# Query and key projections of later batches from fp32r parts instead of fp32

## The reference, cut to what matters

```
Q = (query @ Wq.T + bq)          # query = layernorm(x)
K = (key @ Wk.T + bk)            # key = context
scores = einsum('bhqd,bhkd->bhqk', Q, K) / sqrt(16), causal
out = softmax(scores) @ V, then @ Wo.T + bo
x = x + out;   x = x + experts(layernorm(x)) + shared(layernorm(x))
```

## Time and profile before

| | |
|---|---|
| median of three runs | 495.11 us |
| the profiled execution | 494.46 us, its span 492.4 us |
| mean granted TensorE clock | 0.995 of full |
| PE busy, DVE, ACT, POOL | 93%, 63%, 43%, 40% of the span |
| chain that ended last | PE 68%, DVE 15%, ACT 6%, issue 5%, DMA 4% |
| L679, the projections | 64 records; 7% is the largest line of the chain (L628), L679 has 6% |

### The profile page before, as it was taken

How to read it: one execution, slowest core, us unless ns; L and a number is a source line. 1 busy time by engine, 2 the same in 40 slices (tenths; PEclk the granted TensorE clock), 3 DMA queues, 4 the chain that set the end, 5 groups by cost and what they waited for, 6 DMA issues and landing times.

```text
span 492.4 us, 10465 instructions
## 1 busy us (share of the span) xinstructions
PE 457.4 (93%) x3237; PEld 322.0 (65%) x3238; DVE 312.2 (63%) x651; ACT 211.8 (43%) x421; POOL 196.0 (40%) x204
## 2 busy tenths in 40 slices
PE   7979999999999999999978999999999999999992
PEld 6754444654447444564555546699999999999852
DVE  4985757477563856647975895955455555554446
ACT  2255666527572566656764253332332223223210
POOL 4113544214541337302622003036676666665420
PEclk9999999999999999999999999999999999999997
DMA  8593422422124021310398901014444444444389
GB/s 272 101 230 101 126 72 72 140 69 72 63 76 150 32 97 38 115 64 2 98 379 322 327 2 43 0 39 72 76 64 65 74 75 64 65 72 68 36 208 333
DMA packets 45575, 53.86 MB, mean 109 GB/s; under 512 B 7760, under 2 KB 41872, under 8 KB 44912
## 3 DMA queue, kind: packets, MB, share of 16 engines
q1 hardware_dynamic: 34320, 39.77, 25.2%
q0 software_dynamic: 7488, 10.31, 13.3%
q10 hardware_dynamic: 3744, 3.47, 2.7%
HBM read 27.09 MB, written 13.67 MB: 83 GB/s over the span
## 4 chain that ended last, share of the span: by engine, by line
PE 68%; DVE 15%; ACT 6%; issue 5%; DMA 4%; SPq 1%; POOL 0%; DVEq 0%; ACTq 0%; POOLq 0%
PE set_a L628 7%; PE set_b L658 6%; PE set_a L679 6%; PE set_a L934 6%; PE set_a L933 6%; PE set_a L935 6%; PE set_b L648 4%; DVE attention L1317 3%; ACT attention L1084 3%; PE set_b L952 3%; PE set_a L670 3%; PE set_a L842 3%; PE set_b L953 3%; PE set_b L954 3%; PE set_b L943 2%
## 5 line engine op out<-in xcount | busy, mean ns | idle before, releaser
L1317 DVE TENSOR_REDUCE attention<-set_a 128x2 f32<-128x1024 f32 (+2 forms) x96 | 95.9, 1040 | 25.1 <-PE set_a L630 23.0
L1084 ACT ACTIVATE attention<-set_b 128x512 f32<-128x512 f32 (+1 forms) x176 | 87.8, 570 | 50.2 <-PE set_b L648 36.6
L532 POOL TENSOR_SCALAR_AFFINE_SELECT attention<-attention 128x512 f32<-128x512 f32 x64 | 42.6, 679 | 100.5 <-ACT attention L1084 100.5
L592 POOL DMA_INDIRECT sum_rows<-moe,token_of x39 | 61.8, 1585 | 43.9 <-issue 29.8
L648 PE MATMUL set_b<-attention 99*128 99x512 bf16 (+3 forms) x256 | 59.2, 303 | 7.1 <-ACT attention L1084 5.7
L628 PE MATMUL set_a<-attention 96*128 96x512 bf16 (+3 forms) x256 | 60.5, 302 | 4.9 <-DVE attention L1317 4.7
L1184 ACT ACTIVATE moe<-set_a 128x384 f32<-128x384 f32 x39 | 19.1, 490 | 105.2 <-PE set_a L935 95.6
L584 POOL DMA_INDIRECT e_x<-normed_rows,token_of x39 | 39.4, 1011 | 61.3 <-DVE token_of L1516 34.9
L1541 DVE TENSOR_TENSOR moe<-set_a,moe 128x384 f32<-128x384 f32 x39 | 21.7, 557 | 63.0 <-issue 36.3
L628 PEld LDWEIGHTS set_a<-attention 96*128 96x128 bf16 x256 | 24.9, 97 | 44.3 <-DVE attention L1317 17.2
L933 PE MATMUL set_a<-wup_hi,e_xT_hi 128*128 x156 | 53.0, 340 | 0.0
(11 more groups left out here) (169 smaller groups left out, 859.0 us busy)
## 6 DMA issues: line engine op xcount, KB each, us to landing
attention<-attention SPq DMA_DIRECT2D x182, 64.0 KB, 2.6
wup<-in_wupT SPq DMA_DIRECT2D x2, 3072.0 KB, 15.5
sum_rows<-attention SPq DMA_DIRECT2D x2, 2048.0 KB, 13.0
wup<-sum_rows SPq DMA_DIRECT2D x8, 512.0 KB, 7.4
attention<-in_ctxT SPq DMA_DIRECT2D x7, 512.0 KB, 5.6
w_down<-in_wdnT SPq DMA_DIRECT2D x3, 1024.0 KB, 4.9
x_res<-in_x SPq DMA_DIRECT2D x4, 512.0 KB, 6.5
out<-x_res ACTq DMA_DIRECT2D x8, 256.0 KB, 4.0
```

What stands on the lines that cost most here:

```text
L592: g.indirect_dma_start(acc[i], bass.IndirectOffsetOnAxis(token_of[:, t:t + 1], 0), e_y[:, t % 2, :], None, compute_op=ALU.add).then_inc(ad ...
L1084: nc.scalar.activation(pT[k][:, h:h + heads, :], bank(par)[:, 0:heads * (S - k * P)], ACT.Exp).then_inc(b_free, 1)
L1317: v.tensor_reduce(dst, src, AX.X, ALU.max, negate=True).then_inc(a_free, 1)
```

## The change

- Five of the six halves (all but the first, half 0 of batch 0's loop turn) use `project_parts`: for each chunk c, three fp32r products, so 12 matmuls of 128 x 128 by 128 x 512 for queries and keys together, in place of 4 fp32 ones.
- High parts of the rows are made by ACT copies (`rows_high`): batch 1's together with the weights' after the first slot's exponentials, batch 2's ahead of `part1` in slot 3 of batch 0, batch 3's behind slot 0's exponentials. They lie where `w_down_hi` will be, the weights' parts in the last third of `w_down_lo`.
- Low parts are made by POOL subtractions (`rows_low`), written over the fp32 rows: batch 1's behind the masks of slot 1 of batch 0, batch 2's behind those of slot 3, batch 3's behind those of slot 0. The weights' come ahead of all of these.
- PE waits for the low parts (`in_low`) ahead of each such half. The loops of PE, ACT and POOL over batches run from 1 to 2, with batch 0 written out ahead of them.

```diff
+        in_lo = attention_r[:].rearrange("p (a c n) -> p a c n", a=2, c=C)
+        in_hi = wdn_hi[:].rearrange("p b n -> p (b n)")
+        wqk_parts = wdn_lo[:, M - 1, :].rearrange("p (i a c n) -> p i a c n", i=2, a=2, c=C)
...
+            def low_parts(count, dst, src, high):
+                pool.wait_ge(in_high, count)
+                g.tensor_tensor(dst, src, high, ALU.subtract).then_inc(in_low, 1)
+            def rows_low(b):
+                for a, src in enumerate((xnT, cT)):
+                    low_parts(2 * b + a + 1, in_lo[:, a, :, b * S:(b + 1) * S], src[:, :, b * S:(b + 1) * S],
+                              in_hi_of(b, a))
+            def batch(b, first=False):
                 for s in range(NG):
                     mask_group(B_ATT + b * B_PER + s * B_SLOT, split={0: 2 * b + 2, 2: 2 * b + 3}.get(s))
                     if s == 1:
                         add_bo(b)
+                    if first and s == 0:
+                        pool.wait_ge(val_ready, 3)
+                        rows_low(1)
+                    if first and s > 1:
+                        rows_low(s)
+            for a, w in enumerate((wq, wk)):
+                low_parts(a + 1, wqk_parts[:, 1, a], w, wqk_parts[:, 0, a])
+            batch(0, True)
+            with pool.Fori(1, B - 1) as b:
+                batch(b)
...
+            def project_parts(par, a, half, b):
+                cols = slice(half * P, (half + 1) * P)
+                for c in range(C):
+                    high, low = (wqk_parts[:, i, a, c, cols] for i in range(2))
+                    rows_hi = in_hi[:, bass.ds((b - 1) * (2 * C * S) + (a * C + c) * S, S)]
+                    rows_lo = in_lo[:, a, c, bass.ds(b * S, S)]
+                    mm(pair(A, par)[:, a, :], high, rows_hi, start=c == 0, stop=False)
+                    mm(pair(A, par)[:, a, :], high, rows_lo, start=False, stop=False)
+                    last = mm(pair(A, par)[:, a, :], low, rows_hi, start=False, stop=c == C - 1)
+                return last
...
+                        else:
+                            pe.wait_ge(in_low, 4 + 2 * b)
+                            project_parts(par, 0, half, b + 1)
+                            project_parts(par, 1, half, b + 1).then_inc(a_full, 1)
...
+            def rows_high(b):
+                for a, src in enumerate((xnT, cT)):
+                    copy(in_hi_of(b, a), src[:, :, b * S:(b + 1) * S]).then_inc(in_high, 1)
...
                     if g != 2 and not final:
+                        if first and g == 3:
+                            rows_high(2)
...
                     n, par = exps(n, par, (NG - 1, count + NG - 1), 1)
+                    if first:
+                        rows_high(3)
...
+            for a, w in enumerate((wq, wk)):
+                copy(wqk_parts[:, 0, a], w).then_inc(in_high, 1)
+            act.wait_ge(ld_ctx, DMA * (B - 1))
+            rows_high(1)
```

More of the change, by code:

```diff
@@ L128, in build @@
         REGION = 140 * KB
+        with nc.sbuf_tensor("attention_parts", [P, 2 * C * N], F32R) as attention_r:
+            pass
         with nc.sbuf_tensor("attention", [P, REGION], F32) as attention:
@@ L193, in build, with in_hi_of @@
         zeros = part(D + WHO)
+        in_lo = attention_r[:].rearrange("p (a c n) -> p a c n", a=2, c=C)
+        in_hi = wdn_hi[:].rearrange("p b n -> p (b n)")
+        wqk_parts = wdn_lo[:, M - 1, :].rearrange("p (i a c n) -> p i a c n", i=2, a=2, c=C)
+        assert M == B - 1 and E * D == 2 * C * S == 4 * C * D
+        def in_hi_of(b, a):
+            return in_hi[:, ((b - 1) * 2 + a) * C * S:((b - 1) * 2 + a + 1) * C * S].rearrange("p (c n) -> p c n", c=C)
         xs = [attn, attnT.rearrange("p c (k d) -> p (c k) d", d=D)]
@@ L252, in build @@
         mean_done = sem("mean_done")
+        in_high, in_low = sem("in_high"), sem("in_low")
         val_ready, part1_ready, rem_ready, part2_ready, parts_ready = (sem(n) for n in
@@ L540, in _ @@
             pool.wait_ge(xs_ready, B)
-            with pool.Fori(0, B - 1) as b:
+            def low_parts(count, dst, src, high):
[6 more added lines that the diff above has]
+            def batch(b, first=False):
                 for s in range(NG):
@@ L774, in logits_t, with batch @@
                 return tr(A[:, 2, b * P:(b + 1) * P], lgT[:, b * P:(b + 1) * P], ident[:])
-            def batch(b, final):
+            def batch(b, final, first=False):
                 n_a, par_a = A_PRO + b * A_PER, A_PRO
@@ L783, in projection @@
                         pe.wait_ge(a_free, n - 1)
-                        project(par, 0, half, b + 1)
-                        project(par, 1, half, b + 1).then_inc(a_full, 1)
+                        if first and half == 0:
+                            project(par, 0, half, b + 1)
+                            project(par, 1, half, b + 1).then_inc(a_full, 1)
+                        else:
+                            pe.wait_ge(in_low, 4 + 2 * b)
+                            project_parts(par, 0, half, b + 1)
+                            project_parts(par, 1, half, b + 1).then_inc(a_full, 1)
                     return None if final else projection
@@ L846, in batch @@
                     pe.wait_ge(a_free, n_a)
-            with pe.Fori(0, B - 1) as b:
+            batch(0, False, True)
+            with pe.Fori(1, B - 1) as b:
                 batch(b, False)
@@ L1131, in _ @@
             exps(B_GRP0, B_GRP0, None, 1)
-            with act.Fori(0, B - 1) as b:
+            for a, w in enumerate((wq, wk)):
+                copy(wqk_parts[:, 0, a], w).then_inc(in_high, 1)
+            act.wait_ge(ld_ctx, DMA * (B - 1))
+            rows_high(1)
+            batch(0, False, True)
+            with act.Fori(1, B - 1) as b:
                 batch(b, False)
```

## The result

The changed kernel takes 492.96 us (median of 11 runs, 491.85 to 493.5), the kernel before 495.58 in the same comparison (11 runs, 494.91 to 499.74). The ratio is 0.9933, with a 95% interval of 0.991 to 0.9956: a gain of 0.4 to 0.9%, 3.3 us in the middle, 2.6 between the medians. The ratio is that of the means, and two long executions of the kernel before (498.83 and 499.74 us) make its 3.3 larger than the 2.6 of the medians. The forecast was 494.0, in a range of 491.8 to 496.0; the time lies inside, on the better side. That it would be "no change that can be told" from 0.5% was the wrong side of a narrow line, and the gain of 2.6 is more than twice the 1.1 that was forecast.

A forecast was written before the change was run, and what follows sets the result against it. PE, busy 93%, was taken as the bound, with projection halves on the attention stage's chain. Shorter halves 2.75 us less the hold's 1.66 give 1.1 less, from 495.11 to 494.0; range 491.8 to 496.0.

The forecast's parts named there:

- The half: PE's projection half: 12 fp32r products of 0.233 us, 2.86 in slot 3, 0.63 less than before.
- Rival B: PE's 512-column product takes 0.214 us, half 2.57: 493.3 us, chance 0.12; with A's small hold 491.8, chance 0.05.
- Slot 1: Slot 1 of batches 1 and 2: DVE's tail of the batch before lets only 0.43 us pass, twice.
- The hold: POOL's subtractions hold DVE's row-maximum steps in batch 0, making PE's L638 late: 1.01 plus 0.65, 1.66 us together.
- the spare: End of batch 0: L638 0.97 us late, 0.32 covered because ACT releases PE's next work later, 0.65 stays.
- What was costed at nothing: ACT's copies, PE's wait for the low parts and batch 3's subtractions on POOL: no cost.
- A: DVE goes through its four steps in a row, hold costs 0.16: 2.6 us less, 492.5, chance 0.15.
- C: One POOL subtraction takes 3.34 us in place of 2.38: 2.9 us more, 498.0, chance 0.07.
- D: Behind the shorter half PE waits for something else, only the hold stays: 1.66 us more, 496.8, chance 0.06.

The follow-up runs named there:

- e3: Changed kernel with POOL's row subtractions moved away from the ends of the slots: 492.2 us, ratio 0.9914; again 491.74 us, ratio 0.9912.
- e1: Kernel before with only batch 0 written out ahead of the loops of PE, ACT and POOL: 495.53 us, ratio 0.9982.
- e4: Changed kernel without the product of weights' high and rows' low part, 8 matmuls a half in place of 12: 491.34 us, ratio 0.9901.
- e2: Changed kernel with all parts made and waited for, but the five halves again 4 fp32 matmuls: 496.37 us, ratio 1.0007.
- e5: Changed kernel with 176 of 2048 columns taken out of POOL's subtraction pairs for batches 1 and 2 and done elsewhere: 492.5 us in one run.
- e6: Changed kernel with an extra 176-column subtraction in front of POOL's pairs for batches 1 and 2: 495.69 us in one run.

## Why the prediction was right or wrong

**The half: right.** 12 products of 0.233, 2.87 in slot 3 against 2.86 forecast. Three of them gave 1.93 us (0.66, 0.64, 0.63 in e3 against e1), forecast 1.89. Rival B's product of 0.214 is out.

**Slot 1: mechanism right, limit too tight.** Counted from M3, the half of slot 1 ends 0.63 earlier, as forecast (14.99 in e1, 14.36 in e3). The forecast let 0.43 of that pass, since L1265 could start at 104.52 + 0.05. The 0.05 was for the handing over. Behind a running DVE record there was none: L1327 started 0.09 before that record's end, so 0.55 passed, twice: 1.11 us in place of 0.86. e4 shows that the limit is real: nothing more would pass.

**The hold: mechanism right, price twice too high.** Forecast 1.66, measured 0.86. The rows show three causes.
- POOL's pair ended 0.55 behind the moment when the cast could start, not 0.70, and the turns took 1.47, not 1.52; L669 was 0.82 late at both places, forecast 1.01 and 0.97.
- The step that failed is "It stands in PE's order ahead of the last two score groups and the projection, so all of it is on the path". Being next in PE's order is not being on the path. PE had a wait for ACT between those two groups, and 0.22 of the delay went into it (e2 against e1; 0.23 between e3's and the changed kernel's records).
- At the end of the batch the same wait was counted as work: "from L638 to its next work it takes 1.00" holds the 0.3 for ACT, so the spare was not 0.32 but 0.53 (M3-M4 of e3 against the changed kernel).

0.58 and 0.28 stay, in place of 1.01 and 0.65.

**What was costed at nothing: right but for one.** ACT's copies cost nothing, PE's wait for the low parts is nowhere in the trace, and batch 3's subtractions cost nothing: with them and batch 2's in the tail of batch 0, e3 gains 0.56 in M3-M4, as much as in slot 1 of the next batch, where none runs. Writing out the batch gave 0.04 in the attention, but some 0.36 more outside the span (e1), where the forecast kept the 2.1 of before.

**The rivals.** A (DVE's steps in a row) named the time best, 492.5, by a mechanism that the rows refute: DVE did take turns. B is out by the product's step. The range reached below 493 for A and B alone, so that the time lies inside it is in part luck. C is out, with POOL's subtractions at 2.3 each (4.67 for two). D is out, since the halves passed on.

**Sum.** Forecast 2.75 - 1.66 = 1.1. The stretches between M0 and M11 say 3.07 - 0.86 + 0.04 = 2.25, which is what they differ by: 0.8 from the hold's price and 0.3 from the halves more than forecast. With the 0.36 outside the span it is 2.6, and so far apart are the medians, though they scatter by some tenths.

What happens ahead of M0 stays open. The prologue differs between executions by up to 1.9 us: the first half ends at 47.09 in the profile before and at 49.02 after, with the granted clock at 0.50 of full in the stretch from 30 to 32 us of the latter and not of the former. All seven traces of kernels with halves from fp32r parts have that fall (0.50 to 0.53) and M0 at 57.38 to 57.84; the three with fp32 halves (before, e1, e2) haven't, and M0 is at 55.89 to 56.15. So the fall may belong to the change; but it can't stand in every execution of the one kernel and in none of the other, since the medians would then be at least 1.2 us closer. How often either has it no run here tells. The late start of the attention is why the two profiled executions differ by 0.96 only.

## What to carry to other kernels

A late instruction costs what is left after the next wait on the same engine: before a delay is put on the path, follow the engine on to its next stall in the old trace, and take that stall off. Where work is added on POOL, look at what DVE does in small dependent steps at the end of the new instruction; moving POOL's subtractions off the ends of two slots gave back 0.86 us here, of 3.07. And a product that gets shorter should be checked against the other engine that must take its result: in slot 1 the same change had 0.55 to give and no more.

## What the runs showed of the hardware

- Turns depend on what is ready: DVE's small steps took 0.55 to 0.64 each while POOL had a ready instruction for each turn (the changed kernel), and 0.17 as soon as a mask had to wait for ACT (e5).
- The clock's fall in e6 came after PE had idled 1.32 us (1.00 granted until 69, 0.83 in the next microsecond, 0.50 in the three after it), and it cost 1.58 us, nearly three times the delay that had been added. At the end of the same batch PE idled 1.30 us in the same way and the clock stayed at 1.00 (94 to 95); with idle times of 0.74, in the changed kernel, it stayed at 1.00 too. What tells the two apart isn't seen in these rows.
